# Relation stage: sum products split around a score half, and the first term of the weighted sum on ScalarE

## What is computed

```python
q = (inst_feature[sub] @ Wq.T + bq).reshape(-1, HEADS, DK)      # 8 heads of 64
k = (inst_feature[obj] @ Wk.T + bk).reshape(-1, HEADS, DK)
att = ((q * k).sum(-1) / np.sqrt(DK)).T
scores = jnp.zeros((HEADS, n, n)).at[:, sub, obj].set(att)       # 0 where a pair isn't listed
scores = jnp.where(mask[None], -jnp.inf, scores)                 # mask: not in the adjacency
scores = scores.at[:, di, di].set(1e-07)                         # the diagonal
attn = jax.nn.softmax(scores, axis=2)
aggregator_factor = attn.sum(axis=0) / HEADS
return aggregator_factor @ inst_feature
```

## Time and profile before

| | us |
|---|---|
| median of the timed runs (4329.33 to 4334.23) | 4329.72 |
| profiled execution | 4338.02 |
| its span | 4336.3 |
| TensorE busy | 3594.6 (83%) |
| VectorE busy | 3571.6 (82%) |
| ScalarE busy | 2553.4 (59%) |
| GpSimd busy | 1425.2 (33%) |
| mean granted clock of TensorE | 0.91 |

### The profile page before, as it was taken

The page is one execution under the profiler, slowest core; times in us unless marked ns, Lnnn a source line. Parts: engine busy times, 40 slices in busy tenths (PEclk is TensorE's granted clock), DMA queues, the critical chain, the costliest instruction groups (busy, mean ns, idle before and its releaser), DMA issues. The chain is left out here.

```text
span 4336.3 us, 55622 instructions
## 1 busy us (share of the span) xinstructions
PE 3594.6 (83%) x20081; PEld 2079.6 (48%) x20136; DVE 3571.6 (82%) x5848; ACT 2553.4 (59%) x3008; POOL 1425.2 (33%) x1417
## 2 busy tenths in 40 slices
PE   6888889879788848687887889899988968888887
PEld 3688888634344424243343344677764423333333
DVE  4799999769999996699999925899984079998996
ACT  3566666459888885588897723454443344444442
POOL 0444100007887795399988811000002000000000
PEclk9999999989998969899898899999999978888888
DMA  4611100221110100511101043000002121111110
GB/s 149 246 29 27 29 29 22 67 55 46 46 45 28 34 20 22 168 39 42 29 20 42 17 135 137 24 18 16 19 21 89 40 83 39 49 44 44 44 44 15
DMA packets 160245, 228.82 MB, mean 53 GB/s; under 512 B 85137, under 2 KB 96288, under 8 KB 154672
## 3 DMA queue, kind: packets, MB, share of 16 engines
q1 hardware_dynamic: 148592, 191.33, 13.7%
q0 software_dynamic: 11376, 33.76, 2.1%
HBM read 158.48 MB, written 66.47 MB: 52 GB/s over the span
## 5 line engine op out<-in xcount | busy, mean ns | idle before, releaser
L1695 DVE SCALAR_TENSOR_TENSOR junk<-expd,mid 128x2048 bf16<-128x2048 f32 x440 | 1036.5, 2356 | 13.8
L579 ACT ACTIVATE steepz<-s1b,thr_h 128x1024 bf16<-128x1024 f32 (+1 forms) x768 | 669.9, 927 | 484.3 <-DVE mask L646 471.4
L732 PE MATMUL acc<-V,mask 128*128 128x198 bf16 (+1 forms) x5504 | 747.1, 274 | 121.8 <-DVE mask L646 70.0
L1595 ACT ACTIVATE junk_s<-expd,nmid 128x2048 bf16<-128x2048 f32 x264 | 528.9, 2003 | 130.0 <-POOL nmid L1655 116.4
L732 PEld LDWEIGHTS acc<-V,mask 128*128 128x128 bf16 x5504 | 478.7, 99 | 190.3 <-DVE mask L646 78.9
L1598 ACT ACTIVATE junk_s<-expd,nmid 128x2048 bf16<-128x2048 f32 x264 | 528.0, 2000 | 0.0
L2140 PE MATMUL psS<-KT,qs 64*128 64x512 f32 x1024 | 382.3, 740 | 156.7 <-DVE m L2250 152.3
L739 PE MATMUL acc<-V,adjT 128*128 128x99 bf16 (+1 forms) x5504 | 453.0, 220 | 0.0
L646 DVE TENSOR_TENSOR mask<-steepz,adjT 128x1024 bf16<-128x1024 bf16 (+1 forms) x768 | 398.1, 552 | 11.3 <-PE acc L732 4.5
L739 PEld LDWEIGHTS acc<-V,adjT 128*128 128x128 bf16 x5504 | 368.8, 99 | 49.8 <-issue 1.4
L1467 PE MATMUL psX<-parts,block 128*128 128x512 bf16 x1481 | 354.6, 393 | 13.5 <-DMA block<-adj_dram 10.7
(11 more groups left out here) (306 smaller groups left out, 5800.5 us busy)
## 6 DMA issues: line engine op xcount, KB each, us to landing
rows<-in_adj_dram SPq DMA_DIRECT2D x32, 1024.0 KB, 5.1
s1b<-sT_dram SPq DMA_DIRECT2D x32, 512.0 KB, 3.8
block<-adj_dram SPq DMA_DIRECT2D x32, 512.0 KB, 4.4
adj_dram<-adjT POOLq DMA_DIRECT2D x4, 2048.0 KB, 20.6
rel_table<-zeros POOLq DMA_DIRECT2D x64, 128.0 KB, 19.3
y_dram<-yo SPq DMA_DIRECT2D x32, 256.0 KB, 2.0
step_dram<-xo SPq DMA_DIRECT2D x32, 256.0 KB, 2.0
A<-step_dram SPq DMA_DIRECT2D x8, 1024.0 KB, 13.5
```

What stands on the lines that cost most here:

```text
L579: act.activation(steepz[:, m % RELUS, :], s1b[:, q % 4, :], ACT.Relu, bias=thr_h[:, u, 1, j:j + 1], scale=STEEP).then_inc(relu_ready, 1)
L732: mm = pe.matmul(acc[:, c % 2, i // TB, o:o + 2 * W], mask[:, j % RING, tile(i)], V[:, u, j, 0:2, :].rearrange("p s w -> p (s w)"), start= ...
L1595: act.activation(junk_s[:, 0, :], expd[:, slot[i], :], ACT.Relu, bias=col(nmid, i), accum_out=col(above, i)).then_inc(sums_ready, 1)
L1695: link(dve.scalar_tensor_tensor(junk[:, :], e, col(mid, i), e, ALU.is_gt, ALU.mult, accum_out=col(mass, i)))
```

## The change

Three things, all in `relation_stage`:

1. `apply` gets a third argument: its four products are issued as two and two. The first two now stand between the transposes and the second score half of a pair, the last two behind that half. The waits of `apply` (for `xo_ready` and for the copy of the transposed blocks) now come ahead of the first two.
2. The first term of the weighted sum, `attn = edge * om`, leaves VectorE's `weights` and becomes `plain(t)` on ScalarE, between the small exponentials and `count(t + 1)`. It waits for a new semaphore `own_ready`; VectorE's first weighing waits for `plain_used`.
3. `masks` is cut in two. The diagonal and `rel` stay at the end of the step; `veil` and the second `edge` product move to a new `veils`, which stands behind `weights` in the next step and ahead of the first weighing.

```diff
-                def apply(t, gp):
-                    if gp == 0 and t >= 1:
+                def apply(t, gp, half):
+                    if gp == 0 and half == 0 and t >= 1:
                         pe.wait_ge(xo_ready, t)
                     pe.wait_ge(t_copied, 4 * t + gp + 1)
-                    for j in range(4 * gp, 4 * gp + 4):
+                    for j in range(4 * gp + 2 * half, 4 * gp + 2 * half + 2):
                         mm = pe.matmul(psO[:, :], attnT[:, j, :], nat[:, j, :], start=(j == 0), stop=(j == NT - 1))
-                    if gp == 3:
+                    if gp == 3 and half == 1:
                         mm.then_inc(o_ready, 1)
...
                             transposes(t - 2, m)
+                        if t >= 2 and m >= 1:
+                            apply(t - 2, m - 1, 0)
                         if t < NT:
                             scores(t, m, 1)
                         if t >= 2 and m >= 1:
-                            apply(t - 2, m - 1)
+                            apply(t - 2, m - 1, 1)
                     if t >= 2:
-                        apply(t - 2, 3)
+                        apply(t - 2, 3, 0)
+                        apply(t - 2, 3, 1)
...
+                def plain(t):
+                    act.wait_ge(own_ready, t + 1)
+                    if t >= 2:
+                        act.wait_ge(t_ready, 4 * (t - 1))
+                    act.activation(attn[:, t % 2, :], edge[:, t % 2, :], ACT.Copy,
+                                   scale=om[:, t:t + 1]).then_inc(plain_used, 1)
...
                         act.activation(ed[:, :], nm[:, u, :], ACT.Exp, bias=std[:, 0:1]).then_inc(exps_ready, 1)
+                        plain(t)
                     if t + 1 < NT:
                         count(t + 1)
...
-                    link(dve.tensor_tensor(rel[:, u, :], edge[:, u, :], rel[:, u, :], ALU.mult))
+                    dve.tensor_tensor(rel[:, u, :], edge[:, u, :], rel[:, u, :], ALU.mult).then_inc(rel_made, 1)
+
+                def veils(t):
+                    u = t % 2
+                    dve.wait_ge(rel_made, t + 1)
                     link(dve.tensor_scalar(veil[:, :], rel[:, u, :], -1.0, BIG, ALU.add, ALU.mult))
                     dve.tensor_tensor(edge[:, u, :], edge[:, u, :], rel[:, u, :], ALU.subtract).then_inc(masks_made, 1)
...
+                    dve.wait_ge(own_ready, t + 1)
                     link(dve.scalar_tensor_tensor(y[:, :], nat[:, t, :], own[:, t:t + 1], psO[:, :],
...
-                    link(dve.tensor_reduce(own[:, t:t + 1], wd[:, :], AX.X, ALU.add))
-                    if t >= 2:
-                        dve.wait_ge(t_ready, 4 * (t - 1))
-                    dve.tensor_scalar(attn[:, u, :], edge[:, u, :], om[:, t:t + 1], None,
-                                      ALU.mult).then_inc(plain_used, 1)
-                    dve.wait_ge(plain_used, t + 1)
+                    dve.tensor_reduce(own[:, t:t + 1], wd[:, :], AX.X, ALU.add).then_inc(own_ready, 1)
...
                 def weigh(t, h):
                     u = t % 2
+                    if h == 0:
+                        dve.wait_ge(plain_used, t + 1)
...
                 masks(0)
+                veils(0)
                 for t in range(NT + 1):
                     if t >= 1:
                         weights(t - 1)
+                        if t < NT:
+                            veils(t)
                         weigh(t - 1, 0)
                         weigh(t - 1, 1)
```

More of the change, by code:

```diff
@@ L2082, in relation_stage @@
             masks_made = self.sem(st, "masks_made")
+            rel_made = self.sem(st, "rel_made")
+            own_ready = self.sem(st, "own_ready")
             plain_used = self.sem(st, "plain_used")
```

## The result

| | before | changed |
|---|---|---|
| median of 8 timed runs, us | 4330.04 | 4314.09 |
| lowest to highest, us | 4327.24 to 4336.25 | 4307.53 to 4321.5 |
| ratio, 95% interval | | 0.9963 (0.9953 to 0.9974) |
| profiled execution, us | 4338.02 | 4313.35 |
| its span, us | 4336.3 | 4311.6 |

The account below looks back on a forecast made before the run. VectorE was taken to set the pace, with TensorE making it wait once a step through half clock and queue order. Terms: -44.2 + 13 x 1.0 + 7.3 = -23.9 us, giving 4305.8 us, range 4291 to 4328.

Parts of the forecast that it names:

- The old wait: VectorE's wait for pair 2's first score half, 3.29 us in a late step: all 44.2 us forecast to go.
- (3,1): Pair 3's second score half: ready within 0.3 us of VectorE's wish, counted as no wait.
- A new wait before the scores (1,1): VectorE waiting for pair 1's second score half: 1.0 us in each of 13 steps, range 0.5 to 2.35.
- the 24: Forecast gain of the whole change: 23.9 us off the median.
- T = 4.4 us: Time from TensorE's restart after its gap until its clock comes back, taken between 3.4 and 5.44 us.
- the constant of 1.2: Microseconds subtracted from half the clock's return time to give the new wait for pair 1's second score half.
- Step 2: Pass t = 2, where tile 0 has no `xo` to wait for: TensorE without a gap, no wait counted.
- W+16.3: 16.3 us after the step's first weighing starts: TensorE's clock was forecast to fall again about there.
- the rival of the slower end: Low clock delays both score halves, TensorE's gap at the step's start grows: +19 us, 4349 us; chance 10%.
- The rival of the full clock: TensorE's clock stays full through the gap before `xo`, no new wait: -36.9 us, 4292.8 us; chance 10%.
- The ScalarE product: edge x om on ScalarE: first weighing 0.44 us later in 15 tiles, 0.71 us in the last; +7.3 us.
- part (b): edge x om moved from VectorE to ScalarE, with masks made in two halves: forecast to cost 7.3 us.

Follow-up runs that it names:

- e9: The kernel before, with all four sum products of a pair ahead of its second score half; ratio 1.0069, median 4360.5 us.
- e3: The kernel before, with the sum products split two and two and finish(t-3) issued ahead of weigh(t-1, 3); ratio 0.9900, median 4286.9 us.
- e4: The changed kernel, with finish(t-3) issued ahead of weigh(t-1, 3); ratio to before 0.9919, median 4295.3 us.
- e5: The kernel before, with only finish(t-3) issued ahead of weigh(t-1, 3); ratio 0.9992, median 4330.2 us.
- e10: The kernel before, with one sum product ahead of the second score half and three behind it; ratio 0.9899, median 4290.6 us.
- e8: The changed kernel with finish(t-3) ahead of weigh(t-1, 3) and masks made whole again, product still on ScalarE; ratio to before 0.9932, median 4302.6 us.
- e2: The changed kernel with its sum products put back together behind the second score half; ratio to before 1.0002, median 4331.7 us.
- e1: The kernel before, with only the sum products split two and two around the second score half; ratio 0.9959, median 4311.5 us.

## Why the prediction was right, point by point

- **The old wait goes.** Right: 44.2 us to none before the scores (2,0), and none before (3,1), where 0.3 us had been allowed for. e9 shows that with four products ahead this last place becomes a limit.
- **A new wait before the scores (1,1), set by xo, the two products and the scores at low clock.** Right in place and cause (e3, e4: gone with the earlier `xo`; e5: the earlier `xo` is nothing by itself). Its size was forecast as 1.0 us in 13 steps, 13.0 us; it was 20.5 us over 14. This term is where the 24 became 16. Of T = 4.4 us and the constant of 1.2, the first was nearly right (5.0, 6.1 and 3.3 in the three steps shown, 2.8 to 6.2 and in the mean 4.5 over all 13) and the second was too large: the waits are T/2 less 0.7 to 0.8. Two products wholly at half clock take 3.71 us (4028.18 to 4031.89) and not 3.4, and VectorE starts 0.15 us after the scores end (4034.49 to 4034.64), not 0.04; these two make up about 0.27 us of the difference of 0.4 to 0.5, and the rest is open. Step 2, counted at nothing, had a wait of 0.87 us.
- **How the clock got low.** Right in six of the 13 steps, wrong in seven. I had it fall anew at about W+16.3, in a gap of 2.77 us before `xo`. So it did in steps 5, 7, 8, 10, 13 and 15, at W+15.8 to W+16.3 in a gap of 2.78 us. In the other seven it had fallen earlier, in the first step shown at W+4.3 (4016.11), in TensorE's gap at the step's start, which grew from 3.69 to 5.86 us as the rival of the slower end had it, and did not come back before `xo`. At low clock the scores (1,0) and the transposes end so late that the gap before `xo` is only 0.53 us. The sum survives, since it only needs the clock to be low at `xo`; but these seven steps, which go by a path that the forecast hadn't counted, carry 13.2 of the 19.6 us of waits in steps 3 to 15. The rival of the full clock is refuted: in each of the six steps that reach the gap at full clock, the clock fell in it. e10 shows the same fall in most of its steps. What makes a step go one way or the other isn't shown.
- **The ScalarE product costs 0.44 us a tile and 0.71 in the last.** Nearly right: 0.47 at the turn (6.62 against 6.15), 0.52 a step between e3 and e4, and 7.6 us in all against 7.3. ScalarE's pass takes 2.003 us (1.99 assumed). VectorE's 20.6 us of saved work brought nothing, as forecast, since the two mask operations now stand in its place, and where they stood VectorE waits 1.64 us for the exponentials. The Trainium skill's rule (ScalarE: Activation LUTs, Rules for kernel authors), to leave plain multiplications on VectorE, is borne out by e3 against e4 and e8: 7.6 and 13.0 us.
- **The parts add up.** Only partly right, and not asked for in the forecast. In the old order part (b) is free (e2), in the new one with its waits it costs 4.9 us (e1 against the changed kernel), without waits 7.6.
- **The sum by rows of one execution.** -44.2 + 20.5 + 7.6 = -16.1 us; the stage's time fell by 17.8 and the median by 16.0. Taken by experiments, the split alone gives -22.7 (before to e1) and part (b) on top of it +4.9 (e1 to the changed kernel).

**What stays open.** Why the steps of before settle at 51.20 us, and keep that length when the turn takes 0.5 us more or VectorE has 1.3 us more work. It probably lies with TensorE, as its scores end the wait in all of them, and the return of its clock lies 3.1 to 4.5 us before that end in each; but no run changed the clock by itself, so this is argued and not shown. Filling TensorE's gap at the step's start, so that the clock does not fall there, was not tried, nor was one product ahead (e10) together with the earlier finish.

## What to carry to other kernels

Before an instruction is moved ahead in a queue, look for the wait that it brings along: here the two products carried `xo_ready` in front of the scores that VectorE wanted, and issuing the producer of `xo` one VectorE operation earlier was worth 20 to 23 us of stage time on top, more than the change itself (17.8). Taking one product fewer along (e10) brought the same whole time. Work taken off an engine pays only if what it waits for next comes earlier as well: 20.6 us of VectorE work went and the time grew by up to 7.6 us, because the product needed a value that is ready only just before it is used. And when a part of a change measures nothing, ask whether a wait has absorbed it: the same part cost 0, 4.9 and 7.6 us beside a wait of 3.3 us a step, one of 1.6 and none.

## What the runs showed of the hardware that I had not expected

A loop of two engines can settle on a length that does not depend on VectorE's work, within limits: 51.20 us with VectorE's wait at 3.29, 3.25, 2.84 and 1.97 us. With the split alone the waits alternate instead, 0.95 and 2.2 us, the same in two runs. And the same code ahead of the stage ended anywhere from 3482.7 to 3494.6 us in the thirteen profiled executions, 12 us apart. The two executions of the split alone differ by 5.5 us in span (4309.8 and 4315.3), nearly all of it ahead of the stage; the stage by itself repeated to 0.2 us (821.4 and 821.2).
